# Storing the last quarter of an embedding tower's output in two parts of 128 tokens for both batches, instead of one part of 256 tokens with a transfer per batch

## The reference

```
h = h + ffn(layernorm(h))

gate_scores = x @ Wg + bg
mask = one_hot(top_k(gate_scores, 2)).sum(-2)
hid  = gelu(einsum('td,edh->teh', xf, W1) + b1)
y    = einsum('teh,ehd->ted', hid, W2) + b2
out  = einsum('ted,te->td', y, mask)
```

## Time and profile before

| | us |
|---|---|
| median of three runs | 179.95 |
| the profiled execution | 179.91 |
| its span (what the profile covers) | 178.2 |
| PE busy | 148.4 |
| DVE busy | 121.8 |
| ACT busy | 76.2 |

### The profile page before, as it was taken

One profiled execution on the slowest core, in us unless ns is written; L12 is line 12 of the kernel. 1 busy time (PEld: TensorE's weight loads), 2 busy tenths in 40 slices (PEclk: granted clock), 3 DMA queues, 4 the chain that ended last, 5 costly groups with the idle time before them and its releaser, 6 DMA issues.

```text
span 178.2 us, 2298 instructions
## 1 busy us (share of the span) xinstructions
PE 148.4 (83%) x782; PEld 89.1 (50%) x782; DVE 121.8 (68%) x348; ACT 76.2 (43%) x126; POOL 15.4 (9%) x41
## 2 busy tenths in 40 slices
PE   0659999998990595798895999978999999789991
PEld 0355565525790212746774935636657454443430
DVE  6977796589788898999898998993324485031011
ACT  2001153374476532873962013726322745635540
POOL 4022220316100440000000000000000000000000
PEclk9999999999997556659998559999999999999999
DMA  5899953000000000000000000000000000002011
GB/s 147 277 393 361 390 233 89 34 0 0 0 4 0 0 0 0 0 4 0 0 4 0 0 0 0 6 0 0 0 4 0 0 0 0 0 4 59 0 29 29
DMA packets 7138, 9.20 MB, mean 52 GB/s; under 512 B 2388, under 2 KB 4436, under 8 KB 7128
## 3 DMA queue, kind: packets, MB, share of 16 engines
q1 hardware_dynamic: 7128, 9.07, 15.1%
HBM read 8.55 MB, written 0.52 MB: 51 GB/s over the span
## 4 chain that ended last, share of the span: by engine, by line
PE 57%; DVE 33%; issue 4%; ACT 4%; POOL 0%; DVEq 0%; ACTq 0%; POOLq 0%
PE bank L925 9%; PE bank L909 5%; PE bank L619 5%; PE bank L571 4%; PE bank L910 4%; PE bank L597 3%; DVE q_sc L1208 3%; DVE invpos L986 2%; PE bank L774 2%; PE bank L610 2%; PE bank L831 2%; PE bank L825 2%; DVE q_sc L1215 2%; DVE onehot L1010 1%; PE bank L686 1%
## 5 line engine op out<-in xcount | busy, mean ns | idle before, releaser
L558 ACT ACTIVATE hid<-bank 128x512 f32<-128x512 f32 x32 | 17.9, 599 | 21.4 <-PE bank L910 21.3
L571 PE MATMUL bank<-spin 128*128 128x512 bf16 x68 | 18.8, 422 | 0.4 <-DVE score L1320 0.4
L925 PE MATMUL bank<-hid,ffn_sb 128*64 128x512 f32 x64 | 16.8, 614 | 0.0
L1335 DVE TENSOR_TENSOR h<-bank,h 128x256 f32<-128x256 f32 x4 | 1.7, 422 | 21.7 <-PE bank L936 21.7
L909 PE MATMUL bank<-xp,w1hi 128*128 128x512 f32 x32 | 14.7, 458 | 0.4 <-ACT xp L542 0.4
L910 PE MATMUL bank<-xp,w1lo 128*128 128x512 f32 x32 | 12.6, 395 | 0.0
L571 PEld LDWEIGHTS bank<-spin 128*128 128x128 bf16 x68 | 7.1, 112 | 10.1 <-issue 4.9
L1020 DVE TENSOR_TENSOR dist_sb<-dist_sb,mask_in 128x1024 f32<-128x1024 f32 x8 | 9.4, 1221 | 3.2 <-POOL mask_in L341 3.2
L1233 DVE TENSOR_TENSOR dist_sb<-bank,early_sb 128x256 f32<-128x256 f32 x16 | 6.0, 420 | 7.8 <-PE bank L779 6.9
L909 PEld LDWEIGHTS bank<-xp,w1hi 128*128 128x128 f32 x32 | 6.0, 188 | 8.6 <-ACT hid L558 4.4
L619 PE MATMUL bank<-dist_sb,neigh 128*64 128x512 f32 x32 | 8.6, 660 | 0.0
(11 more groups left out here) (266 smaller groups left out, 336.3 us busy)
## 6 DMA issues: line engine op xcount, KB each, us to landing
dist_sb<-in_dist SPq DMA_DIRECT2D x4, 1024.0 KB, 11.0
mask_in<-in_mask SPq DMA_DIRECT2D x4, 256.0 KB, 10.2
ffn_sb<-in_ffn SPq DMA_DIRECT2D x1, 816.0 KB, 10.9
fold_sb<-in_folded SPq DMA_DIRECT2D x1, 772.0 KB, 12.5
late_sb<-in_late SPq DMA_DIRECT2D x1, 728.5 KB, 11.5
mask_in<-in_mrows SPq DMA_DIRECT2D x1, 512.0 KB, 4.2
out<-h SPq DMA_DIRECT2D x8, 64.0 KB, 1.7
early_sb<-in_early SPq DMA_DIRECT2D x1, 391.0 KB, 3.1
```

What stands on the lines that cost most here:

```text
L558: nc.scalar.activation(hid[:, at % HB], bank[hid_bank[at % 3]][:, :], ACT.Gelu).then_inc(S["hid_set"], 1)
L571: nc.tensor.matmul(bank[i][:, :], spin[:, 0:P], spin[:, :], start=True, stop=True)
L925: mm = nc.tensor.matmul(bank[2][j * D:(j + 1) * D, :], K["e_w2"][:, (e + j) * D:(e + j + 1) * D], hid[:, (at + j) % HB], start=False, stop ...
```

## The change

The last half (g = 1, k = 1) is put out in two parts, n = 0 and n = 1, each of one block of 128 tokens for both batches, 256 columns of bank 2. ACT copies each with an instruction of its own and a signal of its own. PE transposes two blocks of columns for each part, the first part into bank 5 and the second into bank 6; before that it waits for the two results of group 0, which were read from bank 6. DVE adds each part with two additions of 128 elements a partition. SP stores each part with one transfer that goes to both batches: 128 tokens x 64 in each. The number of transfers is eight as before. The other three halves run as before; `output` only takes the bank, the count it waits for and the tiles as arguments.

```diff
-            for g in range(NG):
-                for k in range(2):
-                    sp.wait_ge(S["y_set"], 2 * g + k + 1)
-                    for f in range(NH_):
-                        sp.dma_start(out[2 * g + f, 2 * k * P:(2 * k + 2) * P].rearrange("(c p) d -> p c d", p=P),
-                                     h[:, g, 2 * k:2 * k + 2, f]).then_inc(stored, 16)
-            sp.wait_ge(stored, 2 * 16 * B)
+            for g, k in ((0, 0), (0, 1), (1, 0)):
+                sp.wait_ge(S["y_set"], 2 * g + k + 1)
+                for f in range(NH_):
+                    sp.dma_start(out[2 * g + f, 2 * k * P:(2 * k + 2) * P].rearrange("(c p) d -> p c d", p=P),
+                                 h[:, g, 2 * k:2 * k + 2, f]).then_inc(stored, 16)
+            for n in range(2):
+                c = 2 + n
+                sp.wait_ge(S["y_set"], 4 + n)
+                sp.dma_start(out[2:4, c * P:(c + 1) * P].rearrange("f p d -> p f d"), h[:, 1, c]).then_inc(stored, 16)
+            sp.wait_ge(stored, 16 * (6 + 2))
...
-                    nc.scalar.copy(y_t[:, k], bank[2][:, :]).then_inc(S["y_copied"], 1)
+                    if g and k:
+                        for n in range(2):
+                            nc.scalar.copy(y_t[:, k, 2 * P * n:2 * P * (n + 1)], bank[2][:, 2 * P * n:2 * P * (n + 1)]).then_inc(S["y_copied"], 1)
+                    else:
+                        nc.scalar.copy(y_t[:, k], bank[2][:, :]).then_inc(S["y_copied"], 1)
...
+                def last_turn():
+                    pe.wait_ge(S["y_set"], 2)
+                    for n in range(2):
+                        pe.wait_ge(S["y_copied"], 4 + n)
+                        for c in (2 * n, 2 * n + 1):
+                            mm = nc.tensor.transpose(bank[5 + n][:, c * P:(c + 1) * P], y_t[:, 1, c * P:(c + 1) * P], ident)
+                        mm.then_inc(S["yt_mm"], 1)
...
-                turn(1)
+                    turn(1)
+                else:
+                    last_turn()
...
-                def output(k):
-                    dve.wait_ge(S["yt_mm"], 2 * g + k + 1)
-                    yt = bank[turn_bank[g] + k][:, :].rearrange("p (c j d) -> p j c d", j=2, d=D)
-                    tiles = slice(4 * k, 4 * k + 4)
+                def output(k, at, count, tiles):
+                    dve.wait_ge(S["yt_mm"], count)
+                    cols = slice((tiles.start - 4 * k) * P, (tiles.stop - 4 * k) * P)
+                    yt = bank[at][:, cols].rearrange("p (c j d) -> p j c d", j=2, d=D)
...
-                        output(0)
+                        output(0, 4, 3, slice(0, 4))
                     yield
                 if g == 0:
-                    output(0)
-                output(1)
+                    output(0, 6, 1, slice(0, 4))
+                    output(1, 7, 2, slice(4, 8))
+                else:
+                    output(1, 5, 4, slice(4, 6))
+                    output(1, 6, 5, slice(6, 8))
```

## The result

Nine executions of each kernel (the three that gave the 179.95 us are among those of before): 180.32 us median before (179.48 to 180.66) and 179.17 us after (178.25 to 179.81). The ratio is 0.9941, with a 95% interval of 0.9914 to 0.9968: faster, by between 0.3% and 0.9%. The forecast of 179.36 us lies 0.19 us over the median. The ratio says 1.06 us, the forecast said 0.59; the first question is whether that difference belongs to the change.

The account below looks back on a forecast made before the run. The four-engine line behind the last product, then two issues and a landing, bounds the time. The saved issue (0.42 us) and the parts (0.17) give 0.59 us off the 179.95 median: 179.36 us, range 179.05 to 179.80.

Parts of the forecast that it names:

- What bounds the end: After the last product, copy, transposes, two additions, two issues, the second's landing and 0.4 us of closing follow in line.
- something else moved: Sign to look for in the trace after: a last product ending more than 0.1 us away from 173.39.
- The copy: On ACT, two copies of 256 columns at 0.38 us each, overlapping by 0.10 us, replace one of 0.585 us.
- The transposes: On PE, two pairs of 0.445 us each, the first starting 0.06 us after the first copy's end.
- so it costs nothing: PE's new wait for group 0's results, over some 13 us earlier, was taken to add no time.
- The additions: On DVE, four of 0.284 us replace two of 0.42; the last is over at 175.45, 0.17 us earlier.
- The issues: On SP, second issue at 175.48, free of the first by at least 0.05 us; 0.42 us of the gain.
- The landing: The last transfer lands 1.7 us after its issue, as the second of a pair; 1.6 is the least seen.
- rival (b): Last transfer behaves like a pair's first, 0.37 us issue, 1.6 landing: another 0.1 us, 179.26; chance 0.60 together with the forecast.
- The sum: Last issue moves 0.59 us earlier, 0.42 from the issue and 0.17 from the parts; median forecast 179.36 us.
- The scatter: Measurement tells about 0.3%, 0.54 us; three runs before spread over 179.75 to 180.32; chance of faster 0.54.

Follow-up runs that it names:

- e3: Changed kernel's copy, transposes and additions in two parts, but both last transfers by batch behind the last addition, as before: 180.06 us, ratio to before 1.0000.
- e4: Kernel before with only the last two transfers' pattern changed, one per 128-token block for both batches, both behind the last addition: 179.95 us, ratio 0.9999.
- e1: Kernel before, run again without edit: 179.94 us (179.13 to 180.85, 12 runs), ratio to its own 35 executions 1.0009.
- e2: Changed kernel, run again without edit: 179.49 us (178.11 to 180.02, 12 runs), ratio to before 0.9969.
- e5: Changed kernel with the second part's transposes in bank 0 instead of bank 6, without PE's added wait: 179.86 us, one execution.
- e9: Kernel before with its very last transfer issued by ACT in place of SP, nothing cut in two: 179.99 us, ratio 0.9984.
- e10: Changed kernel with second part in bank 0 and DVE adding the first feature half of both parts, then the second: 179.31 us, one execution.
- e7: Changed kernel with PE summing the feature halves by products with stacked identities, leaving DVE one addition per part: 179.53 us, ratio 0.9978.
- e8: As e7, with the second transfer issued by ACT in place of SP: 179.44 us, ratio 0.9967.
- e11: As e10, with the second part's transfer issued by ACT: 179.46 us, ratio 0.9952.

## Why the prediction was right

- **What bounds the end.** Right. The chain behind the last product is one line through four engines: e3 and e4 each undo one half of the change and return to 4.7 and 4.8 us. The last product did end 0.67 us earlier than in the profile of before, which the prediction took as a sign that something else moved; it was the clock in the body, which e1 and e2 show to change from execution to execution in either kernel.
- **The copy.** 0.38 us forecast, 0.375 measured, with the overlap of 0.10 us (both take 0.65 us).
- **The transposes.** Two take 0.42 us where 0.445 was worked out, but they start 0.14 us after the copy and not 0.06. The step that failed is "so it costs nothing" for PE's added wait: it cost 0.06 us net (e5), as it made the wait for the copy an instruction of its own.
- **The additions.** 0.286 and 0.292 us for 0.284, and starts 0.33, 0.20 and 0.32 us apart for 0.32, 0.20 and 0.32. DVE does pay back most of the lead, and the last addition ends 2.13 us after the last product where 2.06 was forecast, the 0.07 being PE's wait. The estimate from the table in "VectorE: DVE Perf Modes" of the Trainium skill, section "The TRN2 errata — SBUF-src ops pay a fixed extra latency per instruction", 0.258 and 0.357 us, was low on both; the measurement decides, and the rows of like shape were nearer.
- **The issues.** Right: the second is free of the first (0.15 us), and its 0.42 us is the largest term. e9 adds a condition that the text had only touched on: the packets need the gap as well.
- **The landing.** 1.7 us was taken and 1.6 is the truth; rival (b) came in. With 0.15 us of idle queue in front (174.73 to 174.88) the issue is the short one. In e10, where the second follows as closely as in the kernel before (0.04 us), it takes 0.47 us and lands after 1.7; in e7, 0.08 us behind, 0.44 and 1.7. The prediction had this gap among its reasons against (b). The short one is worth 0.1 us; why a gap shortens it stays open.
- **The sum.** +0.10 from the landing and -0.07 from PE's wait make 0.62 us of the 0.59 forecast, and the profile shows about 0.6. That the sum fits so well is luck in part: the two misses cancel; the second measurement gives 0.56 us by its ratio, and the groups of equal clock 0.64 and 0.75.
- **The scatter.** The prediction put the chance of "faster" at 0.54 since the effect was no larger than what can be told. It spoke of a spread of three runs and dismissed the clock, since it is 1.00 in the last stretch; it missed that the body's clock makes two groups 1.0 us apart, so that nine executions against nine can be off by nearly the whole effect (the interval of the first ratio is 0.5 us to either side). The first ratio (1.06 us) fits such a draw, on the lucky side: three of the nine executions after were in the group of the higher clock, and the nine before, whose clocks are not on record, had a median of 180.32 us where the 35 in the lower group have 180.13.

## What to carry to other kernels

Behind the last product a kernel is a line of engines, and there the number of things that stand behind the last result counts: a transfer that needn't wait for it should be issued before it, far enough ahead that both its issue and its packets are out of the way. Cutting the computation into parts pays little by itself, as each part brings its fixed time on the slowest engine of the line (0.29 us for half the columns where the whole took 0.42); it is worth it for what it lets start earlier. Where an instruction stands behind two waits, write first the one whose signal comes last. To judge an effect of half a microsecond, compare the stretch that the edit touches in the profiles, and compare executions of like granted clock.

## What the runs showed of the hardware

- Of two waits ahead of an instruction the first written rode on the instruction and the second became one of its own, behind its signal: 0.10 us later on PE (0.14 against 0.04 us; e2 against e5) and 0.06 us on DVE (0.09 against 0.03; e10 against e5).
- The issue of a 64 KB transfer takes 0.372 us and lands after 1.6 us when SP's queue had a gap of 0.15 us before it, and 0.47 us and 1.7 us right behind another (0.04 us). A gap in the own queue is not all of it: from ACT's queue, with nothing ahead in it, the issue took 0.42 us beside or behind one of SP's (e8, e11) and 0.47 us at the same moment as one (e9).
- Two transfers of 64 KB issued at the same moment from two queues moved their packets in 0.7 us together, and the later landed after 1.9 us: with both at work the two queues moved 209 to 216 GB/s, no more than one alone (up to 243), so the packets share what the queues don't.
- The float32 product of e7 (64 columns moved) shows as two instructions of PE, a transpose of 128 x 128 as one; eight of either in a row take 1.09 us.
